# A hybrid attention, feed-forward and state-space block: where a small softplus stands in the vector engine's order

## The reference, cut to what matters

```
x = x + attention(layernorm(x))          # a gated delta rule, computed in matrix form
x = x + feed_forward(layernorm(x))
x = x + state_space(layernorm(x))        # the layer that the change is mostly about
x = x + feed_forward(layernorm(x))

layernorm(x) = (x - mean) / sqrt(var + 1e-5)     # computed as x * rstd + shift, shift = -mean * rstd

state_space(u):                          # per sequence, 4 heads of 64, state 128
    z, xBC, dt = u @ W_in                # widths 256, 512, 4
    xBC = silu(conv4(xBC) + conv_b)      # causal convolution with 4 taps per channel
    dt  = softplus(dt + dt_bias)         # softplus(v) = log(1 + e^v)
    y   = ssd(x, dt, A, B, C) + x * D    # decays exp of sums of dt * A
    y   = y * silu(z)
    y   = y * rsqrt(mean(y^2) + 1e-5) * norm_w
    return y @ W_out
```

## Time and profile before

| | before |
|---|---|
| median of three executions | 834.76 us (832.90 to 836.47) |
| the profiled execution | 835.77 us |
| its span, first to last instruction | 833.7 us |
| mean granted PE clock | 0.953 |
| PE busy | 746.8 us (90%), 5114 matmuls |
| DVE busy | 619.6 us (74%), 1728 instructions |
| POOL busy | 556.2 us (67%), 920 instructions |
| ACT busy | 531.0 us (64%), 1023 instructions |

### The profile page before, as it was taken

The page is one execution under the profiler, slowest core; times in us unless marked ns, Lnnn a source line. Parts: engine busy times, 40 slices in busy tenths (PEclk is TensorE's granted clock), DMA queues, the critical chain, the costliest instruction groups (busy, mean ns, idle before and its releaser), DMA issues. The chain is left out here.

```text
span 833.7 us, 15931 instructions
## 1 busy us (share of the span) xinstructions
PE 746.8 (90%) x5114; PEld 547.7 (66%) x5114; DVE 619.6 (74%) x1728; ACT 531.0 (64%) x1023; POOL 556.2 (67%) x920
## 2 busy tenths in 40 slices
PE   3589999999999897999779799899979999979997
PEld 2578888888888775666644566566645565546665
DVE  3568877787788548888568787887888777668885
ACT  3244344434543236988548788788978688848886
POOL 1567666776677504777724697588758876777775
PEclk9689999999999899999759899999999999999999
DMA  4341131112111102000200000000000000000112
GB/s 126 82 134 46 50 77 34 30 30 48 39 30 30 29 15 102 0 1 0 78 3 7 1 1 9 1 1 5 7 1 1 9 1 1 1 1 27 51 51 77
DMA packets 59996, 25.83 MB, mean 31 GB/s; under 512 B 22288, under 2 KB 59152, under 8 KB 59664
## 3 DMA queue, kind: packets, MB, share of 16 engines
q1 hardware_dynamic: 59920, 24.90, 11.2%
HBM read 15.26 MB, written 9.63 MB: 30 GB/s over the span
## 5 line engine op out<-in xcount | busy, mean ns | idle before, releaser
L1503 DVE SCALAR_TENSOR_TENSOR arena<-bank,convw_sb,arena 128x510 f32<-128x510 f32 (+2 forms) x192 | 142.5, 745 | 31.9 <-ACT arena L973 27.2
L721 POOL TENSOR_TENSOR arena<-arena 128x768 f32<-128x768 f32 x64 | 114.8, 1814 | 12.8 <-ACT arena L1000 12.6
L701 POOL TENSOR_TENSOR arena<-ff,arena 128x512 f16<-128x512 f32 x64 | 73.6, 1159 | 28.7 <-ACT arena L938 26.6
L1970 PE MATMUL bank<-xnT,win_sb 128*128 128x512 f32 x128 | 73.9, 661 | 2.7 <-DVE arena L1503 2.7
L632 POOL TENSOR_TENSOR leafV<-leafV,leaf_tmp 32x14 f32<-32x14 f32 (+6 forms) x224 | 62.4, 278 | 17.6
L830 ACT ACTIVATE ff<-bank 128x256 f32<-128x256 f32 (+2 forms) x80 | 34.0, 424 | 57.6 <-PE bank L1658 35.3
L1324 DVE SCALAR_TENSOR_TENSOR ff<-bank,ff 128x512 f32<-128x512 f32 x96 | 64.5, 684 | 7.3 <-ACT ff L933 6.3
L933 ACT ACTIVATE ff<-bank 128x512 f32<-128x512 f32 x96 | 56.2, 587 | 18.4 <-PE bank L1886 18.0
L815 ACT ACTIVATE xnT<-bank 128x512 f32<-128x512 f32 x34 | 20.3, 597 | 73.3 <-PE bank L1645 73.3
L628 POOL TENSOR_TENSOR leaf_tmp<-leafV 32x14 f32<-32x14 f32 (+6 forms) x224 | 55.8, 249 | 16.4
L994 ACT ACTIVATE arena<-bank 128x384 f32<-128x384 f32 x128 | 59.8, 492 | 9.3 <-PE bank L1990 8.5
(11 more groups left out here) (216 smaller groups left out, 2162.5 us busy)
## 6 DMA issues: line engine op xcount, KB each, us to landing
LT_dram<-arena SPq DMA_DIRECT2D x16, 256.0 KB, 2.3
ff<-R_dram SPq DMA_DIRECT2D x16, 256.0 KB, 2.8
out<-x_all SPq DMA_DIRECT2D x8, 512.0 KB, 3.2
x_all<-in_L_attn_a_x SPq DMA_DIRECT2D x7, 512.0 KB, 5.6
slabs<-in_tables SPq DMA_DIRECT2D x2, 1024.0 KB, 6.0
ff<-in_tables SPq DMA_DIRECT2D x2, 768.0 KB, 4.3
x_all<-in_L_attn_a_x SPq DMA_DIRECT2D x2, 256.0 KB, 3.7
R_dram<-tab SPq DMA_DIRECT2D x2, 256.0 KB, 6.7
```

What stands on the lines that cost most here:

```text
L701: nc.gpsimd.tensor_tensor(of_block(hl[u], j), hidT[u][:, j, :], of_block(hh[u], j), ALU.subtract).then_inc(hl_done[u], 1)
L721: nc.gpsimd.tensor_tensor(score[h], cb[g % 2], hgam[h], ALU.mult).then_inc(score_done, 1)
L1503: nc.vector.scalar_tensor_tensor(acc_of[:, :, s:SEQ], src_of[:, :, 0:SEQ - s], convw_sb[:, r, TAPS - 1 - s:TAPS - s], acc_of[:, :, s:SEQ], ...
L1970: mm(conv_bank[r % 2][:, :], win_sb[:, INNER + r * P:INNER + (r + 1) * P], xnT[b % XNT_SETS][:, :], start=True, stop=True).then_inc(conv_m ...
```

## The change

It has three parts. First, shift_at makes shift one column at a time: four tensor_scalar instructions of 128 x 1, each with the column of rstd as its tensor, the mean as a per-partition scalar and -1 as a constant, in place of one scalar_tensor_tensor of 128 x 4; the last of the four raises the semaphore. It does so in all 28 calls, those of attention too. Second, in the softplus rounds ACT makes |v| and max(v, 0) in front of the exponential, which takes scale -1 instead; DVE's softplus_begin is left only for the first quad. Third, in DVE's rounds the residual and the last taps come in front of softplus_middle, the series is no longer split, and skip(e, 0) stands between softplus_middle and the series.

```diff
+            def softplus_begin(q):            # ScalarE
+                act.wait_ge(z_done, done(QUAD * (q + 1) - 1))
+                act.wait_ge(chain_step, CHAIN * q)
+                nc.scalar.activation(nabs_dt[:, :], z_dt[q % 2][:, :], ACT.Abs).then_inc(chain_step, 1)
+                nc.scalar.activation(relu_dt[:, :], z_dt[q % 2][:, :], ACT.Relu).then_inc(chain_step, 1)
+                act.wait_ge(chain_step, CHAIN * q + 1)
+                nc.scalar.activation(e_dt[:, :], nabs_dt[:, :], ACT.Exp, scale=-1.0).then_inc(e_done, 1)
...
                 if exp_q is not None:
-                    exp_of_quad(exp_q)
+                    softplus_begin(exp_q)
...
                 dve.wait_ge(rstd_done, done(n))
-                nc.vector.scalar_tensor_tensor(shift[u][:, :], mv[u][:, :, 0], -1.0, rstd[u][:, :],
-                                               ALU.mult, ALU.mult).then_inc(shift_done, 1)
+                for t in range(GROUP_TILES):
+                    last = nc.vector.tensor_scalar(shift[u][:, t:t + 1], rstd[u][:, t:t + 1], mv[u][:, t, 0:1], -1.0,
+                                                   ALU.mult, ALU.mult)
+                last.then_inc(shift_done, 1)
...
                 if d is not None:
                     with_bias(d)
-                if begin_q is not None:
-                    softplus_begin(begin_q)
...
                     taps(b, 2)
+                if f is not None and b is not None:
+                    add_residual(f)
+                if b is not None:
+                    taps(b, 3)
                 if begin_q is not None:
                     softplus_middle(begin_q)
-                    softplus_series(begin_q, 0, 3)
-                if f is not None and b is not None:
-                    add_residual(f)
-                if b is not None:
-                    taps(b, 3)
+                if e is not None and e < GROUPS - 1:
+                    skip(e, 0)
                 if begin_q is not None:
-                    softplus_series(begin_q, 3, 6)
+                    softplus_series(begin_q, 0, 6)
                     softplus_end(begin_q)
                 if e is not None and e < GROUPS - 1:
-                    skip(e, 0)
                     skip(e, 1)
```

More of the change, by code:

```diff
@@ L1583, in space_half @@
                     taps(b, 2)
-                if begin_q is not None:
-                    softplus_middle(begin_q)
-                    softplus_series(begin_q, 0, 3)
                 if f is not None and b is not None:
@@ L1591, in space_half @@
                 if begin_q is not None:
-                    softplus_series(begin_q, 3, 6)
+                    softplus_middle(begin_q)
+                if e is not None and e < GROUPS - 1:
+                    skip(e, 0)
+                if begin_q is not None:
+                    softplus_series(begin_q, 0, 6)
                     softplus_end(begin_q)
                 if e is not None and e < GROUPS - 1:
-                    skip(e, 0)
                     skip(e, 1)
```

## The result

The changed kernel takes 842.95 us (median of 13 runs, 839.8 to 847.83); the kernel before, in 13 runs of its own, 836.3. The ratio is 1.0071, 95% interval 1.0053 to 1.0089: 5.9 us slower, 4.4 to 7.4. Forecast were 841.3 us and +6.5.

The account below looks back on a forecast made before the run. PE bounds attention in a closed loop with DVE; DVE paces the state-space rounds, and PE loses clock behind long waits. Attention +5.9, shift -1.1, round 1 +1.2, rounds 5 and 9 -2.5, rounds 6 and 10 +3.0: +6.5, 841.3 us (838 to 845).

Parts of the forecast that it names:

- Shift in attention, +5.9: Attention: four columns add 0.44 us per call on DVE; PE follows 0.36 later in 13 rounds, plus 1.2 elsewhere: +5.9 us.
- rival of cheap columns: Shift everywhere: a column costs only 0.07 us, as without a scalar; total +1.5, 836.3 us; chance 0.13.
- Shift in the state-space rounds, -1.1: Rounds 3, 4, 7, 8: single columns don't stand behind POOL's scores, saving 0.27 us a round, -1.1 us in all.
- rival of waiting columns: State-space rounds: each column waits for what POOL holds, eight rounds lose 1.8 us each: +14, 855 us; chance 0.07.
- ACT's new work, 0: Softplus rounds: |v| and maximum on ACT cost it 0.3 to 0.4 us, hidden in later waits: 0.
- Round 1, +1.2: Round 1: no residual, last taps wait for ACT's first tap so nothing gained, and a new series stall: +1.2 us.
- Rounds 5 and 9, -1.25 each: Softplus rounds 5 and 9: with the new order skip(e, 1) starts 1.25 us earlier, the stall included.
- the stall: DVE's series behind skip(e, 0): the second small step stands 1.1 us while POOL's gate runs (bounds 0 and 1.27).
- Round 6, +1.8: Start of round 6: PE waits 2.9 us before the dt product and loses clock, as in round 2: +1.8 us.
- rival of free gates: Softplus rounds and 6, 10: POOL doesn't hold the series, PE keeps its clock: -0.6 in all, 834.2 us; chance 0.14.
- Round 10, +1.2: Round 10: no dt product, but the same low clock, given two thirds of round 6's loss: +1.2 us.
- PE not following in attention: Attention rival: the loop has unseen slack, only the state-space terms are left, +0.6: 835.4 us; chance 0.07.

Follow-up runs that it names:

- e12: Changed kernel with both scalars of the column instruction as constants, the mean left out of the shift; 839.9 us in one profiled run.
- e11: The kernel of e10 plus 9 filler matmuls on PE before the dt product (rounds 2, 6) and decay rows (round 10); 831.83 us, 0.9915 of before.
- e4: Kernel before with only |v| and maximum moved to ACT in softplus rounds 1, 5 and 9; 837.00 us, ratio 0.9999 to before.
- e1: Kernel before with only the shift written column by column in all 28 calls; 840.78 us, ratio 1.0038 to before.
- e9: The kernel of e5 unchanged, profiled a second time; 836.0 us in one run.
- e7: Changed kernel plus 14 filler matmuls on PE before the dt product (rounds 2, 6) and decay rows (round 10); 839.68 us, 1.0025 of before.
- e6: Changed kernel with the shift as one instruction in all calls; 839.04 us, ratio 1.0013 to the kernel before.
- e8: Changed kernel with the shift as one instruction in attention, columns in the state-space rounds only; 837.58 us, ratio 1.0000 to the kernel before.
- e3: Kernel before with only DVE's new order in the softplus rounds, shift and ACT's work as before; 836.33 us, ratio 0.9980 to before.
- e5: Changed kernel with skip(e, 0), and so POOL's gate, behind the series in rounds 1, 5 and 9; 840.70 us, ratio 1.0034 to before.
- e10: Changed kernel with the edits of e5 and e8 together; 834.09 us, ratio 0.9947 to the kernel before.

## Why the prediction was right, step by step

**Shift in attention, +5.9: right in its mechanism, too large by the rows.** A column costs 0.12 us (0.13 forecast). The rival of cheap columns falls: e12 shows that its price holds only where both scalars are constants. The cover was larger than I took. Behind the slower shift the row sum waits no longer for ACT but only for DVE's own queue, and takes 0.64 instead of 0.69: 0.08 + 0.05 = 0.13. A round costs 0.28 for the forecast 0.36: 4.1 us from the fifth call to the last, not 4.7. Outside them the rows show 0.4, where I put 1.2. So attention is 4.5 us by the rows; the timed pairs give 5.9, 6.7 and 7.3, each within some 2.5, and what they show beyond the rows stays open. It is not the DMA of the start-up. DVE's row for the first transpose of its result, in the changed kernel and in e11, which has the one instruction in attention, reads

```profile
46.36 0.71 DVE L1164 STREAM_TRANSPOSE ff<-ff 128x512 f32<-128x512 f32 x1 [3.38 <-DMA ff<-R_dram]
```

```profile
45.72 0.71 DVE L1168 STREAM_TRANSPOSE ff<-ff 128x512 f32<-128x512 f32 x1 [3.67 <-DMA ff<-R_dram]
```

The wait was 1.18 before and 1.26 in e4, and with columns 0.86 in e1, 0.66 in e9 and 2.79 in e7: short and long ones come with either form.

**Shift in the state-space rounds, -1.1: right.** The pair e6 and e8, which differs in this alone, shows -1.0 in rounds 3, 4, 7 and 8. In the changed kernel they gave -0.5, -0.2, -1.1, -0.2: in round 7 more than the shift moved (round 10 below). The rival of waiting columns falls: 204 ns for each of 40 columns, and at most 215 in all 112.

**ACT's new work, 0: right in rounds 5 and 9, small in round 1.** There it costs 0.3 (e3 against e6 and the changed kernel). That it costs nothing in rounds 5 and 9 hangs on the columns: with the whole shift it is 0.2 to 0.3 in each, through POOL, a way that the prediction did not have.

**Round 1, +1.2.** Between `dt_z` and skip(e, 1) the round is 1.34 us longer, with the gate's hold of one step and the wait for ACT's first tap as described; the order alone makes 1.05 of it (e3), ACT's work 0.29.

**Rounds 5 and 9, -1.25 each.** Both -1.32; the stall forecast at 1.1 was 1.03, and e5 removes it by moving the gate.

**Round 6, +1.8.** +1.98, PE's wait 2.71 for 2.9 forecast. e7 shows that the idle time is the cause. The forecast gave the fall as a consequence of the wait's length, and the rival of free gates a border, "a PE wait of under about 2 us". No such border is in the rows: behind 1.80 us round 6 lost nothing in e5, 1.2 us in e9 and 2.6 in e10. Behind waits of 2.63 to 2.72 it lost clock in all five profiles that have them, but not alike: the dt product ran at full clock in e3 and at low clock in the changed kernel, and the round took 19.9 to 22.4 us (changed, e3, e6, e8, e12). So the forecast had the right side, and +1.8 is a value out of a spread of +1.1 to +3.7.

**Round 10, +1.2: wrong place, nearly right sum.** It is +3.79, three times the forecast: PE waited 2.71 us there too, and low clock lasted from the decay rows at 631.29 to the transposes at 640.84 (mean 0.76). In the other four profiles with that wait it is +2.1 to +3.8, more than round 6 in three of them, so that two thirds of round 6 was the wrong estimate and not only bad luck. Rounds 11 and 12, which I left at nothing, gave back 1.46 and 0.96. The scan at the head of round 11, before and after:

```profile
639.42 2.96 DVE L1475 TENSOR_TENSOR_SCAN ff<-ones_col,ff 32x256 f32<-32x256 f32 x1
```

```profile
652.55 1.50 DVE L1486 TENSOR_TENSOR_SCAN ff<-ones_col,ff 32x256 f32<-32x256 f32 x1
```

It reads two tensors and stands until POOL's two gates end. Before, POOL came to them at 639.36, 1.20 us behind skip(e, 1) at 638.16, since its own work of round 10 ended only then; now at 651.00, 0.28 ahead of skip(e, 1), so the scan stands 1.5 us less. Round 7 has the same scan (1.23 us before, 0.67 now). In round 12 the clock was 1.00 for 0.91, which is not surely the order's: e1, with the old order, has 1.00 there too. Rounds 10 to 12 together: +1.4. The same give-back makes e3 cheaper than I expected of it.

**Sum.** The rows show +4.5 for attention, +1.3 for round 1 and -1.1 for rounds 2 to 12, which is +4.8, for 6.5 forecast; the timing says 5.9, and both lie in its interval, 4.4 to 7.4. Attention is 1.4 under its forecast, the state-space rounds 0.3 (+0.3 for +0.6), these by errors that cancel in rounds 10 to 12. Some luck is in how close the total came. PE not following in attention is refuted by e1, free gates by e3 and e5: the gate held a step, and the clock fell.

## What to carry to other kernels

Four tiny instructions in place of one cost their fixed parts, and where PE waits for that queue in every round PE pays for most of it (0.28 of 0.41 us here): look for slack behind them before splitting, and keep the split only where the whole one stands for POOL. Work that moves a wait of PE from one place to another has not removed it; if it now stands in one block, look at the clock behind it in more than one profile: here blocks of 1.80 us cost clock in round 6 in two of three profiles, of 2.6 us and more in all five. Harmless matmuls in front of the wait kept it (e7, e11). Before placing small dependent steps of two SBUF tensors on DVE, look at what the instruction in front of them sets off on POOL.

## What the runs showed of the hardware

- A DVE tensor_scalar of one column took 0.06 us of its queue with constants and 0.12 with a per-partition scalar (e12, changed kernel).
- It never stood for POOL: 199 to 215 ns in 112 instructions, where the one instruction with two tensors took up to 1.17 us in the same places.
- The same wait of 1.80 us on PE left the granted clock of the round at 1.00, 0.91 or 0.84 (e5, e9, e10), and filler matmuls in front of it kept 1.00 (e11). One profile of such a kernel says little about its median; e5's profiled run was 833.9 us, its median 840.7.
- ACT's 0.3 us of extra work reached DVE through POOL: POOL's scores started later, and a DVE instruction with two SBUF tensors stood 0.90 us for 0.61 behind them (e4).
